# Four strings of turns replaced: the order in which four batch elements share each engine

## Time and profile before

| | |
|---|---|
| runs, median (lowest to highest) | 1735.27 us (1735.03 to 1737.14) |
| span of the profiled execution, first to last instruction | 1734.0 us |
| PE busy, instructions | 1698.0 us, 10006 |
| PE weight loads busy | 1300.6 us |
| DVE busy, instructions | 1234.6 us, 4490 |
| ACT busy, instructions | 1088.9 us, 2904 |
| POOL busy, instructions | 1218.5 us, 1771 |
| mean granted TensorE clock | 0.998 |

### The profile page before, as it was taken

How to read it: one execution, slowest core, us unless ns; L and a number is a source line. 1 busy time by engine, 2 the same in 40 slices (tenths; PEclk the granted TensorE clock), 3 DMA queues, 4 the chain that set the end, 5 groups by cost and what they waited for, 6 DMA issues and landing times.

```text
span 1734.0 us, 31744 instructions
## 1 busy us (share of the span) xinstructions
PE 1698.0 (98%) x10006; PEld 1300.6 (75%) x10006; DVE 1234.6 (71%) x4490; ACT 1088.9 (63%) x2904; POOL 1218.5 (70%) x1771
## 2 busy tenths in 40 slices
PE   8999999999999999999999999999999899999998
PEld 5788888876667676676666677767788787788976
DVE  7864335688987988988899866445566766578773
ACT  6555226556677678777776786446546666665656
POOL 5655649898878987888789785135347876666667
PEclk9999999999999999999999999999999999999999
DMA  7100000010000000000000000000000001000002
GB/s 254 71 29 1 1 2 3 3 51 1 1 1 1 1 1 1 1 1 1 1 1 1 1 11 6 1 1 7 2 3 3 1 18 31 21 1 2 2 2 73
DMA packets 24027, 26.70 MB, mean 15 GB/s; under 512 B 3492, under 2 KB 20772, under 8 KB 23476
## 3 DMA queue, kind: packets, MB, share of 16 engines
q1 hardware_dynamic: 23860, 24.67, 4.4%
HBM read 22.52 MB, written 2.15 MB: 14 GB/s over the span
## 4 chain that ended last, share of the span: by engine, by line
PE 80%; POOL 6%; DVE 6%; ACT 4%; issue 2%; DMA 0%; SPq 0%; POOLq 0%; ACTq 0%; DVEq 0%
PE ps L87 74%; PE ps L90 7%; POOL arena L104 6%; ACT arena L98 4%; DVE arena L104 2%; DVE arena L110 1%; DVE arena L130 1%; DVE arena L147 1%; ACT arena L99 0%; DVE arena L133 0%; ACT L98 0%; DVE arena L107 0%; DMA arena<-in_x 0%; DVE arena L136 0%; DVE ps L147 0%
## 5 line engine op out<-in xcount | busy, mean ns | idle before, releaser
L104 POOL TENSOR_TENSOR arena<-arena 128x512 f32<-128x512 f32 (+6 forms) x836 | 715.5, 869 | 278.4 <-DVE arena L110 96.9
L98 ACT ACTIVATE arena<-ps 128x128 f32<-128x128 f32 (+11 forms) x1204 | 338.6, 326 | 394.1 <-PE ps L87 287.8
L87 PE MATMUL ps<-arena 128*128 128x128 f32 (+4 forms) x2792 | 441.0, 291 | 10.0 <-DVE arena L104 3.5
L87 PEld LDWEIGHTS ps<-arena 128*128 128x128 f32 x2792 | 373.3, 191 | 97.9 <-issue 46.5
L104 DVE TENSOR_TENSOR arena<-ps,arena 128x128 f32<-128x128 f32 (+4 forms) x696 | 312.9, 468 | 176.0 <-PE ps L87 163.6
L98 ACT ACTIVATE arena<-arena 128x128 f32<-128x128 f32 (+1 forms) x836 | 321.2, 439 | 51.3 <-POOL arena L104 39.6
L87 PE MATMUL ps<-arena,moe 128*128 128x256 f32 (+1 forms) x960 | 288.2, 439 | 0.0
L87 PE MATMUL ps<-arena,cst 128*128 128x504 f32 (+2 forms) x768 | 283.6, 489 | 2.2 <-ACT arena L98 1.1
L98 ACT ACTIVATE arena<-ps,cols 128x512 f32<-128x512 f32 x324 | 216.8, 688 | 103.3 <-PE ps L87 96.5
L104 POOL TENSOR_TENSOR arena<-arena,cst 128x144 f32<-128x144 f32 (+7 forms) x536 | 186.2, 356 | 93.0 <-ACT arena L98 57.4
L110 DVE SCALAR_TENSOR_TENSOR arena<-ps,arena 128x128 f32<-128x128 f32 (+1 forms) x476 | 156.6, 364 | 120.4 <-PE ps L87 94.2
(11 more groups left out here) (120 smaller groups left out, 1756.5 us busy)
## 6 DMA issues: line engine op xcount, KB each, us to landing
rows<-in_rows SPq DMA_DIRECT2D x1, 2253.0 KB, 14.2
arena<-in_x SPq DMA_DIRECT2D x8, 256.0 KB, 5.3
wf<-in_wf SPq DMA_DIRECT2D x2, 1024.0 KB, 6.6
arena<-in_L_ffn_W SPq DMA_DIRECT2D x8, 256.0 KB, 2.9
out_dram<-arena SPq DMA_DIRECT2D x8, 256.0 KB, 2.7
wmod<-in_wmod SPq DMA_DIRECT2D x4, 384.0 KB, 7.7
arena<-kept SPq DMA_DIRECT2D x24, 64.0 KB, 2.9
arena<-kept SPq DMA_DIRECT2D x8, 192.0 KB, 3.0
```

Of the source, the lines that this page charges most:

```text
L87: return UNSENT if self.e is None else self.e.matmul(out, lhsT, rhs, start=start, stop=stop)
L98: return self.e.activation(out, in_, func, bias=bias, scale=scale)
L104: return UNSENT if self.e is None else self.e.tensor_tensor(out, a, c, op)
```

## The change

The four strings in `TURNS` (lines 391 to 499) are replaced; nothing else in the program differs. The old strings have 3333, 3861, 2145 and 1180 digits (pe, dve, act, pool), the new ones 3303, 3831, 2115 and 1150, which is exactly the number of steps of each engine; the 30 more of the old ones find exhausted generators. Every element keeps its order within each engine, so each instruction, its operands and its waits are the same ones.

```diff
 TURNS = {
-    "pe": ("2000000000000120002230001222000112200011100211012003013211003031110332001332322330320113213131222121"
-          "1333222011133020000112103211133320042330100300213103322000203332002200300100003001200100032022202021"
...
+    "pe": ("0000002000030020010220002122001012020011102011012031201031000111330332003233201233132221133113121210"
+          "2333222011133020020110103211322311243003300300030302203010223330200201000301002001300102000022221020"
...
-    "dve": ("4000000000000000440111424242222222001122222230011133033303233401000031221110020200113121003111000422202"
...
+    "dve": ("4000000000000014400202102334022032121434211222221231023131101312012000042030100203321001002032222100"
...
```

More of the change, by code:

```diff
@@ new lines @@
+    "act": ("1040444200030202122221110131000323133342112300003030004131102000001002230021302010110203220202320121"
+          "0032003233112211123210112113231211200112123110130312011321113321121201212320010323000130031130210103"
+          "0020313012000003223100001322203130300001211020122302033000210321331311210002220000122211301100012002"
+          "2022321030111332123221320200003312011332122331331020200333310113121301202122302113311101312332222031"
+          "2310333002300001313331110213232202220000312333330111320130031303031313032222122100022020322103332111"
+          "3323111022303233010312121110132222330132103111002010023220131212123333010231202000012213123111030233"
+          "2312223112011100100322330123301031111012022310310332230322002223011131313123021130022201012023032333"
+          "1321301000100130123222200033313200331110212122020130001021010210121100230332101010120110022022121131"
+          "2310302100003032333122022011312333121302302222303300102221111212231000031203121211213210303320133301"
+          "2022221232131133120123101222321210001230323310313122122210303332003130011310331133303122221323102333"
+          "3202301102013123100003023303232121223101000230130120200002022120332031023211100202003203231322220111"
+          "2123313133222320312111211001001021222111312212003002101233332223122032111331113321110022223221000010"
+          "2230030303103003102210031101133303120101032110021102301131203313031020302221013120203023313023200110"
+          "0212332200113021302102330132030333333121121123202011322110322031021320331111301231232212323032002323"
+          "0200232212012220331102331001323210033011030322301323332310020201333330230303310033023133320133220100"
+          "0122110221110122311222213301302022310313011120003031223200313033221011121000300132330330022223323130"
+          "2010313103100121313032122321103322001020123111112123202021133332221121331300312123000332120033113031"
+          "1221323223310133301323001302132301212303321131033022002202102312003132131330121101020333300133303322"
+          "1012203010200023113223310120311313130213213123120021313211332232320312230320010321312320302320213230"
+          "3300221003123211101012030110301232021221102220021123010301302332123310300203211323211212103311112332"
+          "1023321312312230322322332330313303221133321203020000001113231110112322012002110221333233131133222233"
+          "233000232231033"),
@@ new lines @@
+    "pool": ("4020104320123000012000220100130210231310043121010332211013202033011322112331132001212313000000232231"
+          "2013200321033000032030003200002122222112111111120211111010030120002121222111113111323300221113121320"
+          "3212010321300001233102333301201100230230313223320133002222030201232231301332330123130123021200031212"
+          "0213333212301323210331223010032131113203030123303120332220014303213103120312310122031220231213103321"
+          "3013203212013200112013201231332211301102320003120033120322130230111210310013022301301003122210210122"
+          "0231012030101233302323132121002132211300201312303202031221230231111133031300231203132223031320122010"
+          "0203012031202203233010332112301221213012112130213002320301202001000031111311311131123222222322022322"
+          "0333303303103133333333333102200010110000200020201210010121113220213200121032100213223311221122322000"
+          "1201002013300310301033013203230233233013311031102112201131212022312213121232232211133332313301332033"
+          "3032033223310311300010030002100020223001113103310112101011011302221132323033201223233032121303232223"
+          "1213301120010323322010032002301202301110131020331102211222010132221123111332213330232203332033230113"
+          "32130012233031210201212331232233331010102233232130"),
```

143 lines of the change are left out of this document (70 added, 73 removed).

## The result

The changed kernel takes 1748.96 us (1747.69 to 1749.88, 4 runs) against 1735.44 us (1735.03 to 1737.14, 4 runs) beside it: ratio 1.0071, 95% interval 1.0059 to 1.0084. The forecast was 1728 us, the range ended at 1741. So the sign was wrong and the time lies outside.

A forecast was written before the change was run, and what follows sets the result against it. PE was taken to bound the kernel end to end, standing still some 85 us. From 1734.0 us, -4 (short trips) and -3 (own-result waits) gave 1727.0, plus 1.3 for the runs' median: 1728 us, range 1716 to 1741.

The forecast's parts named there:

- No work changes: Whole kernel: every instruction and the order inside each element stay, ACT's table loads stay at 95; 0 us.
- The stagger stays: Elements' stages: none starts or ends more than 9 us of PE work earlier or later; 0 us.
- Uncovered microseconds of short trips are PE's loss: PE's round trips under 1.3 us: the rest not covered by other elements' work falls from 28.1 to 24.3 us; -4 us.
- Fewer own-result waits, -3: DVE, POOL, ACT: fewer steps directly behind their own element's (DVE 288 fewer, 16 us of its time); -3 us at PE.
- Contention of DVE and POOL at 0: Operations side by side on DVE and POOL change; tails of some 5 us, between -2 and +2 at PE, taken as 0.
- Rival D: Slower, 1741 us: in layer 1, busy DVE and POOL queues block PE and gains elsewhere are lost; chance 0.20.
- `l1qkv` to `l1a` +3.3: Layer 1 round trip of PE: its uncovered rest grows from 5.4 to 8.7 us, a loss of 3.3 us.
- `l1p` to `l1qkv` by 1.5: Layer 1 round trip of PE: its uncovered rest grows from 0.5 to 2.0 us, a loss of 1.5 us.
- `e3k` to `e3t` by 1.3: Another PE round trip counted for the slower case: its uncovered rest grows by 1.3 us.
- below 16 us: Sign of a right forecast: PE's visible idle time between 1300 and 1700 us falls below 16 us.
- The head I had at 0: Start of the kernel: the start-up stays as it was, so the new order costs 0 us there.
- Rival B: Large gain, 1715 us: PE's 85 us of stalls come from queues holding ready work behind unready work; chance 0.17.

The follow-up runs named there:

- 41 covers: Kernel before with 41 PE steps moved a few places later, behind other elements' work, to cover short round trips; other engines untouched: 1742.25 us, ratio 1.0038.
- 54 fills: Kernel before with 54 ready PE steps moved ahead of PE steps that waited (55, less one that read unlanded weights); other engines untouched: 1739.59 us, ratio 1.0014.
- layer 1 piece: Kernel before with the new turns of all four engines only for what began between 300 and 1040 us: 1740.24 us, ratio 1.0023.
- spliced kernels: Kernel before with the new turns in one stretch only (0 to 30, 30 to 300, 300 to 1040, 1040 to 1480, 1480 us to end): 1737.07 to 1740.24 us.
- spliced head: Kernel before with the new turns of all four engines only for what began in the first 30 us: 1738.93 us, ratio 1.0016.
- the one with `mcols` moved: Changed kernel with DVE's two common steps that write dec0 and mcols put ahead of element 1's first norm step: 1748.39 us, ratio 1.0067.
- those with a changed head: Changed kernel with DVE's mcols steps moved ahead (1748.39 us), and changed kernel with DVE's old turns in the first 30 us (1746.44 us).

## Why the prediction was wrong, point by point

**No work changes: right.** 10006 matmuls, 92 and 3 table loads (ACT 2904 instructions in both), the same busy times within 0.4%.

**The stagger stays: right but for the common delay.** By the sign that I had named (a stage more than 10 us from its old place) it would be wrong, for the stages start up to 14.9 us later. Less the delay that all elements share at that time, none starts more than 5 us from its old place. Single steps move further: in layer 0's mixture of experts one comes 24.6 us later and another 25.0 us earlier.

**"Uncovered microseconds of short trips are PE's loss": this is the step that failed.** I put 28.1 to 24.3 us at -4, up to -10, and the same growth of the longer trips, +4, at nothing. The piece I was surest of came true at its place: the waits before `l1w` fell by 2.5 us, where 2.6 were forecast. The sum of PE's waits rose by 13.7 us all the same. That such a gain isn't kept, the kernels with 41 covers (+6 us, where the pricing had -11.2) and 54 fills (+0.3 us between 58 and 1674 us) show directly. My reading of it, which fits the waits that grew in both kernels but isn't shown step by step: PE's wait in front of a step isn't a hole beside the path that could be filled; it is the place where PE meets an element's chain that is itself late through DVE, ACT or POOL. Fill it, and PE meets the same chain at its next step. The count behind my term was a count of symptoms.

**"Fewer own-result waits, -3": the mechanism was there, its worth was not.** DVE's steps behind one of their own element fell from 1364 to 1076 as counted; of the exposed own-result waits 108 are gone (470 to 362), 12.9 us of DVE time against 16 forecast (58.8 to 45.9 us). None of it is seen as a gain at PE. The -3 had no firm ground either: the chain's row gave 1 us, and doubled that is 2. A tempting explanation is that the space between two such steps has to be filled with another element's step, which makes each chain longer and PE's waits with it. In the changed kernel, around 397 us, DVE does two elements' chains in turns:

```profile
396.42 0.17 DVE L110 SCALAR_TENSOR_TENSOR arena<-arena,ps 128x16 f32<-128x16 f32 x1
396.51 0.29 DVE L104 TENSOR_TENSOR ps<-ps,arena 128x128 f32<-128x128 f32 x1
396.81 0.18 DVE L110 SCALAR_TENSOR_TENSOR arena<-arena,ps 128x16 f32<-128x16 f32 x1
396.91 0.29 DVE L104 TENSOR_TENSOR ps<-ps,arena 128x128 f32<-128x128 f32 x1
397.23 0.36 DVE L136 RECIPROCAL arena<-arena 128x16 f32<-128x16 f32 x2
397.52 0.49 DVE L104 TENSOR_TENSOR arena<-ps,arena 128x128 f32<-128x128 f32 x2
```

and PE, in the same kernel:

```profile
398.06 0.77 PE L90 MATMUL ps<-cst,arena 128*128 128x128 f32 x5 [0.64 <-DVE arena L104]
```

PE waits 0.64 us in the records, 0.80 from start to start. But the kernel before has the same pieces of work, in the same order on DVE:

```profile
389.67 0.17 DVE L110 SCALAR_TENSOR_TENSOR arena<-arena,ps 128x16 f32<-128x16 f32 x1
389.76 0.29 DVE L104 TENSOR_TENSOR ps<-ps,arena 128x128 f32<-128x128 f32 x1
389.96 0.17 DVE L110 SCALAR_TENSOR_TENSOR arena<-arena,ps 128x16 f32<-128x16 f32 x1
390.05 0.29 DVE L104 TENSOR_TENSOR ps<-ps,arena 128x128 f32<-128x128 f32 x1
390.37 0.36 DVE L136 RECIPROCAL arena<-arena 128x16 f32<-128x16 f32 x2
390.66 0.49 DVE L104 TENSOR_TENSOR arena<-ps,arena 128x128 f32<-128x128 f32 x2
```

```profile
391.09 0.76 PE L90 MATMUL ps<-cst,arena 128*128 128x128 f32 x5
```

The two chains take 1.48 us there (389.67 to 391.15) and 1.59 us in the changed kernel; PE loses 0.31 us from start to start there and 0.80 here. What differs is PE's own queue. Before, it takes first the `l1a` of element 0, whose product DVE finishes first. In the changed kernel it stands at the `l1a` of element 1, finished 0.20 us later, with element 0's behind it, and it is free for it 0.84 us behind the start of DVE's chains, where it was 1.11. These two make up most of the 0.49 us by which the wait grew; DVE's own part is at most the 0.11 us by which its two chains take longer. Over all 128 chunks the `l1a` transposes that wait over 0.06 us went from 8 to 20, their waits from 2.5 to 5.8 us, but DVE's chain from `rec`'s sum to the product didn't get longer: its mean fell from 2.28 to 2.08 us. Over the whole kernel, though, a DVE step whose inputs from elsewhere are there starts 449 ns behind its element's former step in the kernel before and 522 ns in the changed one (some 1970 such pairs). Whether that sits on PE's path no kernel here shows. Which engine's order makes most of the loss stays open.

**Contention of DVE and POOL at 0: right as far as the rows show.** POOL's small powers have 1002/1017/1667 ns at their least, median and most, as in the earlier trace rows. The 48 DVE products have a mean of 248 ns now, not 294, so 2.3 us less of DVE time.

**Rival D had the sign, its terms were right in part.** "`l1qkv` to `l1a` +3.3": the waits before `l1a` rose by 3.3 us (3.2 in the layer 1 piece alone). "`l1p` to `l1qkv` by 1.5": the waits before `l1qkv` rose by 0.7. "`e3k` to `e3t` by 1.3": those before `e3t` stayed at 0.4. What I had as layer 1's price, 3.3 + 1.5 = about +5, is +4.7 in the spliced kernel's trace. That agreement is partly luck, for the gain before `l1w` was kept (1.8 us in that piece), where D had it lost, and small waits before other steps make up for it. I gave D 0.20 because it was the sum of the same kind of terms as my own, and I let the signs of the short trips outweigh the long ones, "most of it hidden behind lengths that are themselves queueing". The largest of these long ones wasn't hidden. Where D was short, 1741 us against 1748.96: it had the loss nearly in layer 1 alone. In the spliced kernels' traces the head costs 1.9 us, 30 to 300 us 3.0, 1040 to 1480 us 1.2 and layer 3 3.0, together twice as much as layer 1. Its sign, PE waiting for DVE in layer 1 more than the 7.6 us of idle before, didn't show: the visible idle there is 6.2 us. So the signs by idle time (this one, and "below 16 us" between 1300 and 1700, where it is 14.1) both spoke for a gain, and only the start-to-start sum spoke for the loss.

**The head I had at 0.** DVE's old and new heads differ in plain sight: the 15th digit of the new string lets element 1's norm step in front, and x is loaded in element order over 10 us, as the DMA queue of the kernel before shows. A step that waits for a DMA, moved ahead of steps that don't, had a price of 1.9 us in three traces (the changed kernel, the spliced head and the one with `mcols` moved), and its sign could have been read off the diff.

**Rival B** (headroom of 85 us, filled by the new order) falls with the fills.

**A reading of the earlier trace rows** was off: PE's row of before has three slices below nine tenths, not four. Nothing rests on it.

No spliced kernel beat the kernel before; of the pieces of the new order the lowest ratio is 1.0005, for 1040 to 1480 us.

## What to carry to other kernels

This schedule, tuned as one piece over four engines, couldn't be judged by counting its waits, and it wasn't improved by filling them singly: 54 fills of ready work moved PE by 0.3 us. Idle time in the records can fall while the kernel gets slower (16.0 to 14.1 us here); pair the instructions of the two traces and look at how late each is. Ask of a reordering which element's chain each queue now holds up, and look first at steps that wait for a DMA and were moved ahead of others. And in this kernel, without loops and with all engines in step, a delay at the start was paid in full at the end (1.95 us after 58 us, 1.92 after 1674), so its first ten microseconds are worth as much as any others.

## What the runs showed of the hardware that I had not expected

**TensorE's clock falls in some executions at a place where it stays full in others.** In the spliced kernel with only the first 30 us changed it fell at 1692.8 us, 1650 us behind the last change; the same stretch of the kernel before, 1.92 us earlier on its clock, stayed at full speed. Stretches of that kernel:

```profile
1688.80:1692.80 4.00, 2.61 (x15) 1.63 (x13) 3.26 (x22) 3.18 (x11) 2.26 (x3) 1.00 0.10 31
1692.80:1696.20 3.40, 3.28 (x9) 2.25 (x10) 1.96 (x12) 1.80 (x5) 0.91 (x2) 0.50 0.37 100
```

and of the kernel before, at the same pieces of work:

```profile
1686.88:1690.88 4.00, 2.62 (x15) 1.64 (x13) 3.26 (x22) 3.18 (x11) 2.26 (x3) 1.00 0.11 28
1690.88:1694.28 3.40, 3.28 (x15) 2.04 (x16) 2.21 (x14) 3.15 (x7) 0.91 (x2) 1.00 0.46 102
```

In the 4 us ahead of it PE did the same 15 matmuls in both, busy for 2.61 and 2.62 us, and the other engines did the same too: what PE did just before doesn't tell the two apart. In the stretch itself PE starts 9 matmuls at half speed and 15 at full. Each such fall of 3.4 us cost 1.4 to 1.7 us here. In the changed kernel the one at 114.6 us came behind 6.5 us in which PE's records show no idle time at all, and two kernels with the same order there (those with a changed head) didn't have it. So of the 13.7 us in the changed kernel's trace some 1.7 are of this kind, and differences of 1 to 3 us between single profiles of this kernel shouldn't be read without a look at the clock.
